# A top-2 expert layer, computed for all tokens or for gathered rows only

## What is computed

```python
# x: (1024, 512) normalized rows; gate_w: (512, 8); expert_w: (8, 512, 512)
logits = x @ gate_w                       # (1024, 8)
top_v, top_i = top_k(logits, 2)           # two experts for each token
w = softmax(top_v)                        # two weights for each token
out[t] = w[t,0] * (x[t] @ expert_w[top_i[t,0]]) + w[t,1] * (x[t] @ expert_w[top_i[t,1]])
# then the layer's output is normalized and added to the residual stream
```

## Time and profile before

| | us |
|---|---|
| median of 3 runs | 1896.18 (1892.11 to 1896.88) |
| profiled execution | 1907.18 |
| its span, first to last instruction | 1905.5 |
| PE busy, whole span | 1713.7 |
| from the first transpose of attention's output (1658.54) to the first expert matmul (1719.85) | 61.3 |
| expert matmuls (1719.85 to 1897.33) | 177.5 |
| after the last expert matmul | 8.2 |

### The profile page before, as it was taken

The page is one execution under the profiler, slowest core; times in us unless marked ns, Lnnn a source line. Parts: engine busy times, 40 slices in busy tenths (PEclk is TensorE's granted clock), DMA queues, the critical chain, the costliest instruction groups (busy, mean ns, idle before and its releaser), DMA issues.

```text
span 1905.5 us, 25672 instructions
## 1 busy us (share of the span) xinstructions
PE 1713.7 (90%) x9030; PEld 1343.0 (70%) x9030; DVE 1311.1 (69%) x2025; ACT 727.2 (38%) x1338; POOL 973.5 (51%) x821
## 2 busy tenths in 40 slices
PE   3699999999999999899999869992899999878998
PEld 2478777877777778777877658781666767647886
DVE  5787888777878778878787755666267767663224
ACT  2443433434434434344343223330266766520110
POOL 3366675776666757767667650016333433161223
PEclk9889999999999999999999879995899999989999
DMA  3001020020010200100102011120000000101101
GB/s 129 1 34 45 1 78 1 0 77 0 33 44 0 77 0 7 70 0 33 44 1 78 1 36 70 66 77 34 0 12 1 13 1 1 46 4 63 44 22 44
DMA packets 16290, 61.31 MB, mean 32 GB/s; under 512 B 5472, under 2 KB 5600, under 8 KB 10976
## 3 DMA queue, kind: packets, MB, share of 16 engines
q1 hardware_dynamic: 16224, 60.44, 8.9%
HBM read 58.34 MB, written 2.10 MB: 32 GB/s over the span
## 4 chain that ended last, share of the span: by engine, by line
PE 70%; DVE 12%; POOL 6%; issue 6%; ACT 4%; DMA 2%; SPq 1%; POOLq 0%; DVEq 0%; ACTq 0%
PE banks L294 40%; PE banks L1426 6%; PE banks L1358 3%; PE banks L1545 3%; PE banks L1436 2%; PE banks L1367 2%; PE banks L1325 2%; PE banks L1504 2%; PE banks L1535 2%; DMA x<-in_w_conv 1%; DVE tap L966 1%; POOL am L551 1%; POOL wol L299 1%; DVE nmax L1189 1%; PE banks L1483 1%
## 5 line engine op out<-in xcount | busy, mean ns | idle before, releaser
L551 POOL TENSOR_TENSOR am<-ah,upto 128x1024 fp32r<-128x1024 f32 x64 | 130.3, 2036 | 227.7 <-PE banks L1325 212.4
L966 DVE SCALAR_TENSOR_TENSOR tap<-banks,parg,tap 128x511 f32<-128x511 f32 (+2 forms) x288 | 214.9, 746 | 29.1 <-ACT tap L733 22.3
L1042 DVE TENSOR_TENSOR em<-em,gmask 128x1024 f32<-128x1024 f32 x64 | 132.5, 2070 | 93.2 <-ACT em L766 92.7
L688 POOL TENSOR_SCALAR kz<-kst,head 128x512 fp32r<-128x512 f32 x64 | 99.1, 1568 | 160.3 <-DVE kst L1173 160.3
L294 PE MATMUL banks<-xTh,wch 128*128 128x512 f32 x384 | 166.3, 433 | 6.1 <-POOL wcl L299 4.7
L551 POOL TENSOR_TENSOR am<-al,upto 128x1024 fp32r<-128x1024 f32 x64 | 159.2, 2488 | 0.0
L294 PE MATMUL banks<-xTh,wcl 128*128 128x512 f32 x384 | 152.4, 397 | 0.0
L294 PE MATMUL banks<-xTl,wch 128*128 128x512 f32 x384 | 151.6, 395 | 0.0
L909 ACT ACTIVATE prob<-banks,nmax 128x128 f32<-128x128 f32 (+3 forms) x256 | 121.8, 530 | 53.9 <-DVE nmax L1189 53.6
L1358 PEld LDWEIGHTS banks<-dtx,em 128*128 128x128 f32 x1024 | 123.2, 192 | 23.0 <-issue 21.3
L1189 DVE TENSOR_REDUCE nmax<-banks 128x2 f32<-128x256 f32 (+3 forms) x128 | 104.7, 818 | 40.1 <-PE banks L1536 39.9
(11 more groups left out here) (244 smaller groups left out, 4622.6 us busy)
## 6 DMA issues: line engine op xcount, KB each, us to landing
x<-in_w_conv SPq DMA_DIRECT2D x7, 1536.0 KB, 6.7
x<-in_w_gate SPq DMA_DIRECT2D x8, 1024.0 KB, 4.7
x<-in_w_out SPq DMA_DIRECT2D x8, 1024.0 KB, 6.8
ew<-in_expert_w SPq DMA_DIRECT2D x8, 1024.0 KB, 4.8
gur<-in_ff_gu SPq DMA_DIRECT2D x7, 1024.0 KB, 4.8
x<-in_hidden SPq DMA_DIRECT2D x16, 256.0 KB, 4.2
dnr<-in_ff_dn SPq DMA_DIRECT2D x7, 512.0 KB, 3.5
out<-x SPq DMA_DIRECT2D x8, 256.0 KB, 2.0
```

What stands on the lines that cost most here:

```text
L551: m = pool.tensor_tensor(am[:, part, :, :], a[:, i, :].bitcast(F32).unsqueeze(2).to_broadcast([P, HG, P]), upto[:, :].unsqueeze(1).to_broa ...
L688: m = pool.tensor_scalar(kz[:, quad % 2, p2, j, :], kst[:, p2, :].bitcast(F32), head[:, j:j + 1], None, ALU.mult)
L966: nc.vector.scalar_tensor_tensor(tap[:, q % 2, sh:L], bk(CONV_BANKS[q % 2])[:, 0:L - sh], parg[:, KC * q + k:KC * q + k + 1], tap[:, q % 2 ...
L1042: nc.vector.tensor_tensor(em[:, s % 2, :, :], em[:, s % 2, :, :], gmask[:, :].unsqueeze(1).to_broadcast([P, HG, P]), ALU.mult).then_inc(m_ ...
```

## The change

The routing of the last layer becomes a list of rows. The steps are:

1. The expert matrices all stay in SBUF. SP loads eight of them (`eraw`) from the end of attention on, into space that attention has left; ACT rounds them and POOL (experts 2 to 6) and DVE (0, 1, 7) make low parts in place. The tiles `xTh`, `xTl` of this layer are not made any more.
2. Each normalized tile of `acc` is stored to a DRAM table `xnd` by SP. PE also transposes it to `xnT` and multiplies by the router, in full float32, with 8 columns for each token tile; these stand between the output products of attention.
3. DVE and PE build the lists. A token and one of its two experts is a pair; there are 2048 pairs. A matmul with ones and a triangle counts the pairs of each expert ahead of a pair; from this comes the pair's slot. Slots stand in tiles of 128 that belong to one expert, 23 tiles at most (2048 / 128 + 7). 16 matmuls turn the slot of each pair into two lists, `row_from` (the row of `xnd` for each slot) and `row_to` (the place of the pair in the DRAM table `yd`). A third list, `expert_of`, is read by PE into registers.
4. POOL gathers the 128 rows of each tile with an indirect transfer (`xg`, eight buffers). PE transposes, ACT and DVE make `xgT`'s parts, PE multiplies by the tile's expert (12 matmuls, the weights' address from a register), ACT copies the product to `yb`, POOL scatters its rows to `yd`.
5. After the last scatter SP reads the two product rows of each token back (`mates`, 512 KB a tile). ACT multiplies the first by its softmax weight, DVE adds the second times its weight, and `norm_round(4, n)` follows.

Some semaphores are merged with others of the same order, constants of the lists are made on POOL during the feed-forward layer, and SBUF is laid out anew. The core of the diff:

```diff
@@ gpsimd
-                with pool.Fori(0, NE // 2) as e:
-                    for s in range(2):
-                        for k in range(KT):
-                            pool.wait_ge(e_hi, 2 * KT * e + KT * s + k + 1)
-                            low(pool, ewl[:, s, k, :], ew[:, s, k, :], ewh[:, s, k, :]).then_inc(e_lo, 1)
+                lows = [(e, k) for e in POOL_LOWS for k in range(KT)]
+                for e, k in lows[:KT]:
+                    expert_low(pool, e, k).then_inc(e_lo_pool, 1)
                 for n in range(ROUNDS):
                     norm_pool(3, n)
+                    expert_low(pool, *lows[n + KT]).then_inc(e_lo_pool, 1)
+                for e, k in lows[KT + ROUNDS:]:
+                    expert_low(pool, e, k).then_inc(e_lo_pool, 1)
+
+                def gather(j):
+
+                    if j >= 4:
+                        pool.wait_ge(rows_in[j % 4], 16 * (j // 4))
+                    pool.indirect_dma_start(xg[:, j % GATHERED, :], None, xnd[:, :], bass.IndirectOffsetOnAxis(
+                        ap=row_from[:, j:j + 1].bitcast(U32), axis=0)).then_inc(rows_in[j % 4], 16)
+
+                def scatter(j):
+
+                    pool.wait_ge(yb_out, j + 1)
+                    if j >= 2:
+                        pool.wait_ge(yd_out[j % 2], 16 * (j // 2))
+                    pool.indirect_dma_start(yd[:, :], bass.IndirectOffsetOnAxis(ap=row_to[:, j:j + 1].bitcast(U32), axis=0),
+                                            yb[:, j % 4, :], None).then_inc(yd_out[j % 2], 16)
+
+                pool.wait_ge(xn_out, 16 * NT)
+                pool.wait_ge(list_ready, 1)
+                for j in range(GATHERED):
+                    gather(j)
+                pool.wait_ge(list_ready, 2)
+                for j in range(SLOT_TILES):
+                    if j + GATHERED < SLOT_TILES:
+                        pool.wait_ge(xg_tr, j + 1)
+                        gather(j + GATHERED)
+                    scatter(j)
@@ scalar
+                for j in range(SLOT_TILES + 1):
+                    if j < SLOT_TILES:
+                        act.wait_ge(xg_tr, j + 1)
+                        if j >= 2:
+                            act.wait_ge(yx_ps, j - 1)
+                        nc.scalar.copy(xgT[:, j % 2, 0, :], bk(j % 2)).then_inc(xg_hi, 1)
+                    i = j - 1
+                    if i >= 0:
+                        act.wait_ge(yx_ps, i + 1)
+                        if i >= 4:
+                            act.wait_ge(yd_out[i % 2], 16 * (i // 2) - 16)
+                        nc.scalar.copy(yb[:, i % 4, :], bk(2 + i % 2)).then_inc(yb_out, 1)
@@ vector
-                norm_vector(3, NT)
+                for n in range(NT, ROUNDS):
+                    norm_round(3, n)
...
+                for n in range(NT * TOP):
+                    nc.vector.tensor_scalar(places[:, n, :], lanes[:, :], lanef[:, n:n + 1], None, ALU.is_equal).then_inc(place_ready, 1)
...
+                for e in DVE_LOWS:
+                    for k in range(KT):
+                        expert_low(dve, e, k).then_inc(e_lo_dve, 1)
...
+                for j in range(SLOT_TILES):
+                    dve.wait_ge(xg_hi, j + 1)
+                    low(nc.vector, xgT[:, j % 2, 1, :], bk(j % 2), xgT[:, j % 2, 0, :]).then_inc(xg_lo, 1)
...
+                    nc.vector.scalar_tensor_tensor(acc[:, i, :], mates[:, i, 1, :], rt[:, 3, i:i + 1], acc[:, i, :],
+                                                   ALU.mult, ALU.add).then_inc(mixed, 1)
+                    norm_round(4, i)
@@ tensor
-                with pe.Fori(0, NE // 2) as e:
-                    for s in range(2):
-                        pe.wait_ge(e_lo, 2 * KT * e + KT * (s + 1))
-                        for i in range(NT):
-                            pe.wait_ge(ex_added, 2 * NT * e + NT * s + i + 1)
-                            products(bk(i), stream(i)(ewh[:, s], ewl[:, s])).then_inc(ex_ps, 1)
+                for j in range(SLOT_TILES + 1):
+                    if j < SLOT_TILES:
+                        pe.wait_ge(rows_in[j % 4], 16 * (j // 4 + 1))
+                        if j >= 2:
+                            pe.wait_ge(xg_lo, j - 1)
+                        for k in range(KT):
+                            m = pe.transpose(bk(j % 2)[:, k * P:(k + 1) * P], xg[:, j % GATHERED, k * P:(k + 1) * P], ident[:, :])
+                        m.then_inc(xg_tr, 1)
...
+                        wh, wl = (t[:, bass.ds(expert_at[i], 1), :, :].rearrange("p e k c -> p (e k) c") for t in (ewh, ewl))
+                        products(bk(2 + i % 2), [(xgT[:, i % 2, 0, k * P:(k + 1) * P], xgT[:, i % 2, 1, k * P:(k + 1) * P],
+                                                  wh[:, k, :], wl[:, k, :]) for k in range(KT)]).then_inc(yx_ps, 1)
@@ sync
+                for n in range(2):
+                    sp.wait_ge(yd_out[n], 16 * len(range(n, SLOT_TILES, 2)))
+                pairs = yd[0:PAIRS, :].rearrange("(c n p) d -> n p c d", c=TOP, p=P)
+                for i in range(NT):
+                    if i >= 2:
+                        sp.wait_ge(back_in[i % 2], 16 * (i // 2))
+                    sp.dma_start(mates[:, i, :, :], pairs[i]).then_inc(back_in[i % 2], 16)
```

More of the change, by code:

```diff
@@ L38 @@
 NE = 8
+TOP = 2
+PAIRS = TOP * NB * L
+SLOT_TILES = PAIRS // P + NE - 1
+GATHERED = 8
 STAGES = 4
```

443 lines of the change are left out of this document (287 added, 156 removed).

## The result

The changed kernel takes 1834.74 us (median of 4 runs, 1831.49 to 1838.63) where the kernel before takes 1894.14 (4 runs, 1891.38 to 1896.88): a ratio of 0.9686, 95% interval 0.9669 to 0.9703. Measured a second time it took 1833.10 (5 runs) against 1894.29, a ratio of 0.9688 (0.9670 to 0.9706). The forecast was 1838. Its profiled execution took 1837.23 us, span 1835.4.

The account below looks back on a forecast made before the run. PE was taken to bound the expert stretch, with chains of short steps around it. Of 99.5 us gained there, 40.9 go back (12.3 before the experts, 8.3 way back, 20.3 rounds): 1896.2 - 58.6 = 1838 us, range 1816 to 1866.

Parts of the forecast that it names:

- attention's last output tile: End of attention: PE's inserted router matmuls and transposes, 4.5 us, of which 1.2 fits into three iterations; +3.3 us.
- to the last normalized tile: After attention's output: 11.6 us before, about 2.1 less without the low parts DVE made in between; 9.5 us.
- router: After the last normalized tile: scaling, four transposes, copy, eight weight loads and semaphores; 5.1 us, logits some 7 us earlier.
- lists: After the router: short DVE steps and counting matmuls in turn, 17.7 us plus 0.6 for waiting on POOL; 18.3 us.
- The tiles: Expert stretch, bound by PE: 276 matmuls instead of 768 at 0.231 us, plus transposes, clock and semaphores; 177.5 becomes 78.0 us.
- Rival C: Expert tiles: register weight addresses or lost clock add 0.05 to 0.1 us a matmul, 14 to 28 us; chance 0.09.
- POOL's transfers: Expert tiles: each indirect transfer taken as 1.3 us, 45 operations, 58 us, hidden under PE up to 1.9 us each.
- Rivals A and B: Expert tiles: POOL's transfers set the pace from 1.9 us each, chance 0.20; whole gain gone at 3.2 us, chance 0.05.
- The low parts on POOL: Rounds of normalized tiles: POOL's 1.3 us low part each round counted at nothing, at worst 1.3 in each of three.
- First slot tile: First gather to first product: gated by DVE's second list, eight low parts (5.4 us) and the rows' low part; 1724.7 to 1732.1.
- Way back, rounds, end: After the tiles: last scatter, landing, load and scaling 8.3 us; seven exposed rounds of 2.9, 20.3 us; end unchanged, 8.2 us.

Follow-up runs that it names:

- The bf16 kernel: Changed kernel with the counting matmuls' ones, triangle and choices in bf16 instead of float32; 1830.98 us, ratio 0.9672.

## Why the prediction was right, point by point

| step | predicted | measured |
|---|---|---|
| attention's last output tile, against before | +3.3 | +3.5 |
| to the last normalized tile | 9.5 | 13.1 |
| router | 5.1 | 6.7 |
| lists | 18.3 | 15.4 |
| first gather to first product | 7.4 | 6.7 |
| first product, against before | +12.3 | +14.1 |
| 23 tiles | 78.0 | 75.75 |
| way back | 8.3 | 7.8 |
| seven rounds | 20.3 | 18.2 |
| end | 8.2 | 10.5 |
| gain | 58.6 | 59.3 |

*The tiles.* The term that carries the result, 177.5 us to 78.0, was off by 2.3 of its 99.5 us. What made it safe was that both ends are PE's own rows: 0.231 us a matmul before, and again after with the weights' address in a register. Rival C is out, with PE busy for 75.71 of 75.75 us and the tiles shorter than forecast.

*POOL's transfers.* The value taken, 1.3, was the nearest row's and is what the trace shows (0.97 and 0.30). That nearness is luck: the row is of arithmetic on 512 columns, and the work here is of another kind. What was no luck was the question asked of it, how long one may take before it shows (1.9 us predicted, 1.85 with the measured room of 83.3 us), and the two kernels with more scatters confirm it from the other side: at 92 transfers the ratio was 0.9895, of the gain only some 20 us left. Rivals A and B were the right ones to fear. That a transfer has a second price, in DRAIN at the program's end, neither the forecast nor a rival had.

*The low parts on POOL.* This is the step that failed: "I count it at nothing, 1.3 in each of three rounds at worst". It looked at whether POOL's own queue delays the square root on which a round hangs. POOL's low part instead reached DVE through the ports: 0.85 to 0.88 us on one scaling in each of seven rounds, 2.7 us up to output tile 7 and 3.1 behind it, 5.8 in all, of which the router's stretch gave 0.8 back. The prediction had the row that shows this, the scaling of 1.48 us in the earlier trace rows, and used it for the last rounds and for the lists, but not for the place where the change puts POOL's low parts beside DVE's scalings. With the port's part, 2.7, and PE's, 0.8, output tile 7 is explained; the +3.3 for PE's inserted work was nearly the right number from the wrong account. To the last normalized tile the stretch was 11.6 us before and is 10.0 without POOL's low parts: the low parts taken off DVE were worth 1.6 where 2.1 was counted, and 3.1 of port came on top where nothing was.

*Router and lists.* Together 22.2 instead of 23.4. The router was mis-sized, 6.7 for 5.1, since the last tile's transposes and router matmuls queue behind those of the tile before it at the low clock (0.50); the last scaling also took 1.48 us beside POOL instead of the 0.54 counted, under that queue. So the logits came 2.6 us earlier than before, and not some 7. The lists were dear only by their counting matmuls, as priced, but less: the 16 records of the eight counting matmuls took 3.6 us (1704.58 to 1708.14) instead of 5.3. No step of the lists was held for 1.2 us like the cast in the earlier trace rows except DVE's two `earlier` operations, 1.28 and 1.16 us, under PE's router. They lie beside POOL's low parts; with those on DVE they took 0.22 and 0.19. The 1 to 2 us that the prediction feared for nearly every list step up to 1711 did not come: POOL's low parts ended at 1703.0, 2.0 us into the lists, and the maximum and index steps before that took what they took in the earlier trace rows. The bf16 kernel shows that 2.9 of this stretch is the data type.

*First slot tile.* The sum was right by 0.7 us, and the gate named was wrong: the eight low parts were done 1 us before the rows' low part was wanted, because a subtraction of that shape on DVE starts every 0.62 us (4.94 for eight) where 0.68 was taken, and the gather took 3.9 us to land. "A gather may take 6 us to land without being seen" left out what follows the landing: transposes (1.12) and ACT's rounding (0.59) stand between it and the rows' low part. With the prediction's own 6.3 us of DVE's work, some 4.5 were covered; with the measured 4.9, which began before the gather, less than 3.

*Way back, rounds, end.* 36.5 instead of 36.8 us. The rounds' 2.86 is the middle value 2.9 between 2.3 and 3.6 that was chosen; the first two, before POOL's first addition, took 1.80 and 2.12. "What follows the last add stays, 8.2" was 2.3 too low: 0.7 of it is the last sum's scaling beside POOL, and 1.6 lies behind the last store's issue (1831.3 to 1835.4, where before had 1903.0 to 1905.5), which is DRAIN ending after the store has landed. This is a term that the prediction did not have: it let the end stay, though the change gives POOL 46 transfers of a kind that it had not issued before.

So the errors cancel: +1.8 before the first product, -2.3 in the tiles, -0.5 and -2.1 behind them, +2.3 at the end. The steps that carry the sum were right in kind, and 1838 against 1834.7 is nearer than the single steps were; that nearness is luck.

Open stays what DRAIN does in its 0.082 us for each indirect transfer, and why the first stores of the result, issued while the last rows are still being read back, take 4.3 to 5.1 us to land in the changed kernel where every later one takes 2.0 to 2.1. They hold nothing up here.

## What to carry to other kernels

When a change puts work on an "idle" GpSimd, ask what VectorE does at that moment: a scaling of 512 columns took 1.41 us beside it and 0.53 without it, and DVE did POOL's addition itself in less time than it had lost to it. Price an operation that no row shows by the point from which it decides (here cover / number of transfers), and look at which row is nearest to that point rather than for the exact price. And when rare tiles are padded for the worst case, the padding has the full price of a tile: 3.2 to 3.4 us each. Count indirect transfers also for the end of the program, where each added 0.08 us to POOL's closing instruction, and let POOL finish its own work early.

## What the runs showed of the hardware

- An indirect transfer of 128 rows of 2 KB keeps GpSimd for 0.97 us (gather 0.947 to 1.531, scatter 0.969 to 1.009) and the next starts 1.27 us after it, two gathers, two scatters or one of each nearly alike (1.25 to 1.30); 92 in a row took 1.29 us each. The first takes 1.53. It lands 3.6 us (gather) and 2.8 us (scatter) after its start.
- POOL's closing DRAIN goes on after POOL's last computation for 0.08 us without indirect transfers and for 3.20, 3.86, 5.74 and 7.62 us with 38, 46, 69 and 92 of them.
- A gather is not held up by a DVE subtraction with both inputs in SBUF. Of the kernel with low parts on DVE, in the tile loop:

```profile
1742.36 1.28 DVE L349 TENSOR_TENSOR ewl<-eraw,ewh 128x512 fp32r<-128x512 f32 x2
1742.80 1.08 POOL L815 DMA_INDIRECT xg<-xnd,row_from  x1 [0.30 <-issue]
```

  The gather that lies under two such subtractions takes 1.08 us instead of 0.97.
- Beside a POOL addition or subtraction with both inputs in SBUF, a DVE scaling of 128 x 512 took 1.27 to 1.48 us instead of 0.53; the bias addition, with one input in PSUM, kept its 0.68.
- 14 records of float32 matmuls of at most 56 columns took 3.10 us at the lower clock (0.50), and 7 records in bf16 0.39 at the same.
- Two loads of 512 KB under way from the scattered table take 4.3 to 4.4 us each in the median and up to 5.4, where 512 KB took 3.5 in the earlier trace rows.
